# Edge stage of a graph layer: padding slots of the edge list get a row number past the table's end, and the row gathers skip them

## The chip, the cores and the metric

The kernel is one program on one core of a Trainium2 chip. The metric is the device time of one execution in microseconds (us). Three runs of the kernel before gave a median of 1887.54 us (1886.41 to 1888.28). All engine names are those of the profile: PE is TensorE's matmuls, PEld its weight loads, DVE VectorE, ACT ScalarE, POOL GpSimd, SP SyncE.

## The reference

A relational graph layer with a gate, then a mixture-of-experts layer (8 experts, top 2). Only the first concerns the change:

```python
# x [1250, 1024]; src, dst, edge_type [21250]; weight [8, 1024, 1024]
x = x + gnn(layernorm(x)); x = x + moe(layernorm(x))

def gnn(x):                                   # R = 8 relations
    out = x @ root + bias
    for r in range(8):
        mask = (edge_type == r)
        sums = segment_sum(x[src] * mask[:, None], dst)
        mean = sums / maximum(segment_sum(mask, dst), 1)[:, None]
        out = out + mean @ weight[r]          # = sum over edges of w_edge * (x @ weight[r])[src]
    z = concat([out, x], 1) @ w_gate + b_gate
    return tanh(out) * z + x * (1 - z)
```

## The kernel before, in words

The program has five blocks, one after the other, with a barrier of all engines between them.

1. The transform (0 to about 936 us). Y = x @ weight[r] for all 8 relations is computed and stored to device memory as a table of 8 x 1280 rows of 1024 floats (row number = relation * NP + node, NP = 1280). Each product is three matmuls, high and low parts in fp32r. Beside it DVE and PE sort the edges by destination block: each block of 128 destination nodes gets a stretch of slots that is padded to a multiple of 256 slots (GROUP = 2 tiles of 128). There are ET = 184 tiles of 128 slots, tile t being column t of `edge_row`, `edge_dst`, `edge_w` and `edge_key`. A slot without an edge is zero in all of them: its row number is 0, its destination number 0 (real ones are 1 to 128). About half way DVE computes these columns in a chain of small steps; then POOL fetches one weight (1/count) per slot with 184 small indirect DMAs from the table INV, and waits for the edge stage.
2. The edge stage (about 938 to 1356 us), the block of the change. Two things are interleaved in an order fixed by the generator `steps()`. "product" steps are four more half-width matrix products (root and the lower half of w_gate), 4 x 80 steps of 3 matmuls. "edges t" steps, one for every 1.7 products, add the rows of edge tile t to the accumulator: POOL gathers the 128 rows of Y that column t of `edge_row` names (one indirect DMA of 512 KB) into one of GR = 5 row buffers `gathered`; ACT multiplies by the edge weight and rounds to fp32r (`ghi`, HR = 3 buffers); DVE makes the rest (`glo`, written in place over the row buffer); PE multiplies both by a selection matrix `sel`, which holds a one where iota (1 to 128) equals the slot's destination number, 4 matmuls a tile; after every second tile DVE adds the result to the block's accumulator.
3. The gate and second layernorm, 4. routing, 5. the experts.

The five buffers are a ring. POOL may issue gather t when PE has finished tile t - 5 (semaphore `edge_tiles_used`), ACT waits for the landing (16 counts on `rows_gathered`), DVE for ACT (`rows_hi`), PE for DVE (`rows_lo`). SP, on its own queue, loads the weights of the next product (512 KB each) and stores the products YX.

The edges per block of destinations, counted from the inputs, are 2146, 2155, 2136, 2195, 2129, 2146, 2252, 2270, 2135 and 1686, together 21250. Blocks 0 to 8 take 18 tiles each and block 9 takes 14, so the blocks fill tiles 0 to 175, and tiles 176 to 183 hold nothing. Of the 23552 slots 2302 (9.8%) are padding. Tiles 17, 35, 53, 89, 107, 161 and 176 to 183 are padding alone, 14 tiles; ten tiles are so in part: 16 (30 of 128 slots), 34 (21), 52 (40), 71 (109), 88 (47), 106 (30), 125 (52), 143 (34), 160 (41) and 175 (106). All padding slots lie in the last partitions of their tile, and in the kernel before each of them fetches row 0 of Y.

Of the kernel before, what the change touches and what calls it, by code (L numbers as in the profile page):

```python
# [10 lines left out]
ALU = mybir.AluOpType  # L11
# [35 lines left out]
def build_program(nc, x, src, dst, edge_type, weight, root, bias, w_gate, b_gate,  # L47
                  gate_w, w1, w2, w3, out):
    s = shapes(x, src, weight, w1, gate_w)
    N, D, R, X, H, NT, NP, KC, HC = (s[k] for k in ("N", "D", "R", "X", "H", "NT", "NP", "KC", "HC"))  # L50
# [4 lines left out]
    assert ET % 4 == 0 and ECOLS >= EFULL + (EREST > 0) and HALF == BANK and D == 1024 and R == 8 and X == 8  # L55
    KEYS = NP * R
    BT = NT * R

    with ExitStack() as ctx:
        banks = ctx.enter_context(nc.psum_tensor("banks", [P, 8 * BANK], F32))  # L60
# [2 lines left out]
        def sem(name):  # L63
            return ctx.enter_context(nc.semaphore(name))
# [33 lines left out]
        edge_row = keep.put("edge_row", [P, ET], I32)  # L98
        edge_dst = keep.put("edge_dst", [P, ET], F32)
# [105 lines left out]
        oh_klo = z2b.put("oh_klo", [P, CPQ, P], BF16)  # L205
        oh_khi = z2b.put("oh_khi", [P, CPQ, BT], BF16)
        placed = z2b.put("placed", [P, 2, ET], F32)
        placed_i = z2b.put("placed_i", [P, 3, ET], I32)
        tfl = z2b.put("tfl", [P, 4, ET], F32)
        inv = z2b.put("inv", [P, BT], F32)  # L210
        YB, PLACE_BANK, COUNT_BANK = 4, psum[6], psum[7]
# [26 lines left out]
        with nc.Block() as block:  # L238
# [114 lines left out]
            def _(dve):  # L353
                v = nc.vector
# [6 lines left out]
                def columns(r, part, first=False):  # L361
# [5 lines left out]
                    def equal(out, n, column):  # L367
                        return v.tensor_tensor(out, iota[:, 0:n].unsqueeze(1).to_broadcast([P, CPQ, n]),
                                               column[:, at].unsqueeze(2).to_broadcast([P, CPQ, n]), ALU.is_equal)
# [6 lines left out]
                    equal(oh_lo[:], P, place_lo)  # L376
                    equal(oh_khi[:], BT, key_hi)
                    equal(oh_klo[:], P, key_lo)
# [129 lines left out]
                step = step1  # L508
                dve.wait_ge(cols_used, 8 * SORT_R)
                step(v.tensor_copy(placed[:], PLACE_BANK[:, 0:2 * ET].rearrange("p (a t) -> p a t", a=2)))  # L510
                step(v.tensor_scalar(inv[:], COUNT_BANK[:, 0:BT], 1.0, None, ALU.max))
                v.reciprocal(inv[:], inv[:]).then_inc(inv_ready, 1)  # L512
# [2 lines left out]
                step(v.tensor_copy(edge_dst[:], placed_i[:, 1]))  # L515
                step(v.tensor_scalar(placed_i[:, 2], placed_i[:, 0], R - 1, None, ALU.bitwise_and))
                step(v.tensor_copy(tfl[:, 0], placed_i[:, 2]))
                step(v.scalar_tensor_tensor(edge_row[:], tfl[:, 0], float(NP), placed[:, 0], ALU.mult, ALU.add))

                step(v.tensor_scalar(tfl[:, 1], iota[:, 0:ET], float(P), None, ALU.mult))  # L520
                step(v.memset(tfl[:, 2], 0.0))
# [4 lines left out]
                step(v.scalar_tensor_tensor(tfl[:, 3], tfl[:, 2], float(R), tfl[:, 0], ALU.mult, ALU.add))  # L526
                step(v.scalar_tensor_tensor(tfl[:, 1], edge_dst[:], float(BT), tfl[:, 3], ALU.mult, ALU.add))
                v.tensor_scalar(edge_key[:], tfl[:, 1], -float(BT), 0.0, ALU.add, ALU.max).then_inc(key_ready, 1)
                with dve.Fori(1 + SORT_R, R - 1) as r:
# [123 lines left out]
        GR, HR, SR, SG = 5, 3, 8, 4  # L653
# [9 lines left out]
        g_in = [sem(f"rows_gathered{i}") for i in range(GR)]  # L663
# [30 lines left out]
        with nc.Block() as block:  # L694
# [31 lines left out]
            @block.gpsimd  # L726
            def _(pool):

                for t in range(ET):
                    if t >= GR:  # L730
                        pool.wait_ge(g_used, t - GR + 1)
                    nc.gpsimd.indirect_dma_start(  # L732
                        out=gath[:, t % GR], out_offset=None, in_=Y,
                        in_offset=bass.IndirectOffsetOnAxis(ap=edge_row[:, t:t + 1], axis=0)).then_inc(g_in[t % GR], 16)

            @block.scalar
            def _(act):
# [885 lines left out]
```

## Time and profile before

| | |
|---|---|
| median of 3 runs | 1887.54 us (1886.41 to 1888.28) |
| the profiled execution, its own time | 1879.97 us |
| its span in the trace | 1877.9 us |
| granted TensorE clock, mean | 0.973 |
| PE busy | 1760.9 us, 94% |
| edge stage, share of the 16 DMA engines | about 83% |

The profile is of one execution. Times in the rows below count from the span's start. A matmul of 512 columns is shown as 0.39 us long although the next one starts 0.23 us after it, since matmuls are pipelined; idle time ahead of a matmul therefore begins only after those 0.39 us. Indirect DMAs are shown on POOL with the time in which their descriptors are written, not that of the transfer; the time from issue to landing is a column of its own.

### The profile page before, as it was taken

The page shows a single profiled execution, that of the slowest core. Times are in us where ns is not written, and L with a number is a line of the kernel's source. Part 1 is how long each engine was busy: PE and PEld are TensorE (multiplying, and loading weights), DVE is VectorE, ACT ScalarE, POOL GpSimd, SP SyncE. Part 2 cuts the span into 40 slices and gives each one's busy share as a digit, 9 for nine tenths or more (in the row PEclk, how much of TensorE's full clock was granted, in tenths as well). Part 3 has the DMA queues.
Part 4 walks back from the last instruction along what each step waited for, and adds up shares of the span by engine and source line. Part 5 has one row for each costly group of instructions (what it writes and reads, how often), then busy time and mean ns, then how long its engine had stood idle before and what let it go on. Part 6 is the DMA issues. An engine that isn't in the chain of part 4 may idle for free. (4 is left out here: it accounts for less than half of the span.)

```text
span 1877.9 us, 22607 instructions
## 1 busy us (share of the span) xinstructions
PE 1760.9 (94%) x8113; PEld 1448.1 (77%) x8113; DVE 962.8 (51%) x1166; ACT 595.3 (32%) x850; POOL 639.2 (34%) x535
## 2 busy tenths in 40 slices
PE   7999999999999999999999999999889967999993
PEld 6888888888888888888777777777668855787882
DVE  8545555655410110010079999998889976434300
ACT  2211111111111111111156656655532212455451
POOL 1000000000166666610055555555355523545531
PEclk9999999999999999999999999999989977999997
DMA  5222222222532222222188888888754445777645
GB/s 199 90 96 90 79 74 73 84 73 79 171 106 92 93 84 90 84 84 89 62 279 265 302 269 294 265 269 281 239 213 168 157 155 197 191 218 187 160 82 152
DMA packets 122552, 292.80 MB, mean 156 GB/s; under 512 B 16084, under 2 KB 32516, under 8 KB 122384
## 3 DMA queue, kind: packets, MB, share of 16 engines
q1 hardware_dynamic: 80592, 161.17, 24.3%
q0 software_dynamic: 41872, 130.44, 23.7%
q8 instruction: 57, 0.93, 0.2%
q14 instruction: 31, 0.25, 0.0%
HBM read 213.92 MB, written 82.76 MB: 158 GB/s over the span
## 5 line engine op out<-in xcount | busy, mean ns | idle before, releaser
L585 PE MATMUL banks<-whi,xhi 128*128 128x512 f32 x1280 | 502.0, 392 | 0.6 <-DVE xlo L473 0.6
L586 PE MATMUL banks<-wlo,xhi 128*128 128x512 f32 x1280 | 498.9, 390 | 0.0
L587 PE MATMUL banks<-whi,xlo 128*128 128x512 f32 x1280 | 498.9, 390 | 0.0
L732 POOL DMA_INDIRECT gathered<-Y,edge_row x184 | 220.8, 1200 | 317.5 <-PE banks L846 180.7
L309 ACT ACTIVATE y_out<-banks 128x512 f32<-128x512 f32 x160 | 95.5, 598 | 717.8 <-PE banks L587 717.8
L358 DVE TENSOR_TENSOR wlo<-w_stage,whi 128x1024 fp32r<-128x1024 f32 x66 | 80.7, 1224 | 459.6 <-ACT whi L301 458.9
L585 PEld LDWEIGHTS banks<-whi,xhi 128*128 128x128 f32 x1280 | 240.8, 188 | 50.6 <-DVE xlo L473 1.2
L587 PEld LDWEIGHTS banks<-whi,xlo 128*128 128x128 f32 x1280 | 240.7, 188 | 50.3
L586 PEld LDWEIGHTS banks<-wlo,xhi 128*128 128x128 f32 x1280 | 240.8, 188 | 49.0
L751 ACT ACTIVATE ghi<-gathered,edge_w 128x1024 fp32r<-128x1024 f32 x184 | 211.3, 1152 | 170.1 <-DMA gathered<-Y,edge_row 164.6
L789 DVE SCALAR_TENSOR_TENSOR glo<-gathered,edge_w,ghi 128x1024 fp32r<-128x1024 f32 x184 | 232.2, 1281 | 42.8 <-ACT ghi L751 42.3
L565 POOL DMA_INDIRECT edge_w<-INV,edge_key x184 | 181.2, 985 | 123.2 <-DMA edge_w<-INV,edge_key 102.6
L845 PE MATMUL banks<-ghi,sel 128*128 128x512 f32 x368 | 147.1, 400 | 19.5 <-DVE glo L789 19.3
L557 POOL DMA_DIRECT2D INV<-inv x1 | 0.6, 563 | 483.8 <-DVE inv L512 483.8
L846 PE MATMUL banks<-glo,sel 128*128 128x512 f32 x368 | 143.7, 390 | 0.0
L827 PE MATMUL banks<-whi,xhi 128*128 128x512 f32 x320 | 125.3, 391 | 3.2 <-PEq L238 3.2
L829 PE MATMUL banks<-whi,xlo 128*128 128x512 f32 x320 | 125.2, 391 | 0.0
L828 PE MATMUL banks<-wlo,xhi 128*128 128x512 f32 x320 | 125.2, 391 | 0.0
L799 DVE TENSOR_TENSOR acc<-acc,banks 128x1024 f32 x92 | 111.7, 1214 | 0.8 <-PE banks L846 0.7
L845 PEld LDWEIGHTS banks<-ghi,sel 128*128 128x128 f32 x368 | 69.0, 187 | 49.9 <-issue 37.1
L1537 PE MATMUL banks<-w13hi,xthi 128*128 x216 | 87.7, 406 | 0.8 <-issue 0.3
L1538 PE MATMUL banks<-w13lo,xthi 128*128 x216 | 85.2, 394 | 0.0
(254 smaller groups left out, 2385.5 us busy)
## 6 DMA issues: line engine op xcount, KB each, us to landing
Y<-y_out SPq DMA_DIRECT2D x160, 256.0 KB, 2.0
w_stage<-in_L_gnn_weight SPq DMA_DIRECT2D x62, 512.0 KB, 3.6
raw<-in_L_ffn_w SPq DMA_DIRECT2D x24, 1024.0 KB, 9.4
YX<-y_out SPq DMA_DIRECT2D x40, 256.0 KB, 5.1
w_stage<-in_L_gnn_w_gate SPq DMA_DIRECT2D x12, 512.0 KB, 7.0
X<-x SPq DMA_DIRECT2D x11, 512.0 KB, 3.0
acc<-in_L_gnn_bias POOLq DMA_DIRECT2D x10, 512.0 KB, 10.3
u<-YX SPq DMA_DIRECT2D x10, 512.0 KB, 5.0
```

The lines of the kernel that those rows point to most:

```text
L565: nc.gpsimd.indirect_dma_start(out=edge_w[:, t:t + 1], out_offset=None, in_=INV, in_offset=bass.IndirectOffsetOnAxis(ap=edge_key[:, t:t + ...
L585: pe.matmul(psum[slot][:], xhi[:, k, at], whi[h][:, k], start=(k == 0), stop=False)
L586: pe.matmul(psum[slot][:], xhi[:, k, at], wlo[h][:, k], start=False, stop=False)
L587: ins = pe.matmul(psum[slot][:], xlo[:, k, at], whi[h][:, k], start=False, stop=(k == KC - 1))
L732: nc.gpsimd.indirect_dma_start(out=gath[:, t % GR], out_offset=None, in_=Y, in_offset=bass.IndirectOffsetOnAxis(ap=edge_row[:, t:t + 1], a ...
L751: nc.scalar.activation(ghi[:, t % HR], gath[:, t % GR], ACT.Copy, scale=edge_w[:, t:t + 1]).then_inc(g_hi, 1)
L789: v.scalar_tensor_tensor(glo[:, t % GR], gath[:, t % GR], edge_w[:, t:t + 1], ghi[:, t % HR].bitcast(F32), ALU.mult, ALU.subtract).then_in ...
L827: pe.matmul(psum[j % 2][:], xhi[:, k, at], whi[0][:, k], start=(k == 0), stop=False)
L828: pe.matmul(psum[j % 2][:], xhi[:, k, at], wlo[0][:, k], start=False, stop=False)
L829: ins = pe.matmul(psum[j % 2][:], xlo[:, k, at], whi[0][:, k], start=False, stop=(k == KC - 1))
L845: pe.matmul(bank[:], sel[:, t % SR], ghi[:, t % HR, cols], start=start, stop=False)
L846: ins = pe.matmul(bank[:], sel[:, t % SR], glo[:, t % GR, cols], start=False, stop=stop)
```

## The change

Two steps are added to DVE's chain and one is altered: `edge_row` becomes relation * NP + source plus 2^20 where the destination number is 0. The gather gets a bound (the last row of the table, 10239) and `oob_is_err=False`, by which indices past the bound are left out instead of being an error. What a skipped slot's partition holds is then what the buffer held before: a finite value, multiplied by the weight of key 0 and selected by nobody, since the slot's destination number is 0. The weight gathers, the number of gathers, tiles and buffers are as before.

```diff
+    NO_ROW = 1 << 20
...
                 step(v.tensor_copy(tfl[:, 0], placed_i[:, 2]))
-                step(v.scalar_tensor_tensor(edge_row[:], tfl[:, 0], float(NP), placed[:, 0], ALU.mult, ALU.add))
+                step(v.scalar_tensor_tensor(tfl[:, 3], tfl[:, 0], float(NP), placed[:, 0], ALU.mult, ALU.add))
+                step(v.tensor_scalar(tfl[:, 2], edge_dst[:], 0.5, float(NO_ROW), ALU.is_lt, ALU.mult))
+                step(v.tensor_tensor(edge_row[:], tfl[:, 3], tfl[:, 2], ALU.add))
...
                     nc.gpsimd.indirect_dma_start(
                         out=gath[:, t % GR], out_offset=None, in_=Y,
-                        in_offset=bass.IndirectOffsetOnAxis(ap=edge_row[:, t:t + 1], axis=0)).then_inc(g_in[t % GR], 16)
+                        in_offset=bass.IndirectOffsetOnAxis(ap=edge_row[:, t:t + 1], axis=0),
+                        bounds_check=R * NP - 1, oob_is_err=False).then_inc(g_in[t % GR], 16)
```

On DVE, in the chain that follows the sort (transform stage), the order before was:

```order
391 L517 CAST tfl<-placed_i 128x184 [waits vector_step]
392 L518 SCALAR_TENSOR_TENSOR edge_row<-tfl,placed 128x184 [waits vector_step]
393 L520 TENSOR_SCALAR tfl<-iota 128x184 [waits vector_step]
394 L521 MEMSET tfl 128x184 [waits vector_step]
```

and in the changed kernel, at the same place, it is:

```order
391 L518 CAST tfl<-placed_i 128x184 [waits vector_step]
392 L519 SCALAR_TENSOR_TENSOR tfl<-tfl,placed 128x184 [waits vector_step]
393 L520 TENSOR_SCALAR tfl<-edge_dst 128x184 [waits vector_step]
394 L521 TENSOR_TENSOR edge_row<-tfl 128x184 [waits vector_step]
395 L523 TENSOR_SCALAR tfl<-iota 128x184 [waits vector_step]
396 L524 MEMSET tfl 128x184 [waits vector_step]
```

Two small instructions are new, each with a wait for the one ahead of it; all that follows on DVE keeps its order. On POOL, PE, ACT and SP the listed instructions and their order are the same. What the list does not show is that the bound is an operand in a register: in the built program one register move now stands ahead of each of the 184 gathers on POOL, and the wait for `edge_tiles_used` is on the move.

## Rows read from the trace of the kernel before

**Rows 1.** The page: busy time of each engine over the span.
```profile
PE 1760.9 (94%) x8113; PEld 1448.1 (77%) x8113; DVE 962.8 (51%) x1166; ACT 595.3 (32%) x850; POOL 639.2 (34%) x535
```
**Rows 2.** Windows over the edge stage: us, then busy (count), clock, DMA share, GB/s.
```profile
938.00:1147.00 209.00, 200.41 (x854) 159.38 (x855) 184.20 (x166) 121.28 (x119) 113.22 (x95) 0.99 0.85 279
1147.00:1252.00 105.00, 99.04 (x426) 78.47 (x425) 94.75 (x86) 60.52 (x60) 57.98 (x47) 1.00 0.85 282
1252.00:1356.00 104.00, 97.69 (x419) 77.31 (x417) 92.89 (x83) 58.77 (x58) 49.63 (x42) 1.00 0.79 257
```
**Rows 3.** Groups by line in 938 to 1356: busy us, mean ns, idle before and releaser.
```profile
L789 DVE SCALAR_TENSOR_TENSOR glo<-gathered,edge_w,ghi 128x1024 fp32r<-128x1024 f32 x184 | 232.2, 1281 | 42.8 <-ACT ghi L751 42.3
L732 POOL DMA_INDIRECT gathered<-Y,edge_row x184 | 220.8, 1200 | 317.5 <-PE banks L846 180.7 <-POOLq L238 130.6 <-issue 6.1
L751 ACT ACTIVATE ghi<-gathered,edge_w 128x1024 fp32r<-128x1024 f32 x184 | 211.3, 1152 | 170.1 <-DMA gathered<-Y,edge_row 164.6 <-PE banks L846 3.7
L845 PE MATMUL banks<-ghi,sel 128*128 128x512 f32 x368 | 147.1, 400 | 19.5 <-DVE glo L789 19.3
```
**Rows 4.** Waits, 938 to 1355: engine line, waited for, total us, times, longest.
```profile
PE banks L845 <- DVE glo L789: 19.3, 26, 2.3
```
**Rows 5.** The row gathers on POOL (ns), and their landing in us (min/median/max).
```profile
L732 POOL DMA_INDIRECT gathered<-Y,edge_row x184: 932/964/2273, 938.7 to 1345.1; - x184
DMA to landing us min/median/max: 4.3/5.8/9.2
```
**Rows 6.** Timeline of POOL, tile 4: start, us, row, idle before.
```profile
944.22 0.94 POOL L732 DMA_INDIRECT gathered<-Y,edge_row  x1 [0.30 <-issue]
```
**Rows 7.** Timeline of PE: first edge matmuls of a tile that came late.
```profile
965.71 0.47 PE L845 MATMUL banks<-ghi,sel 128*128 128x512 f32 x1 [0.85 <-DVE glo L789]
...
984.85 0.47 PE L845 MATMUL banks<-ghi,sel 128*128 128x512 f32 x1 [0.55 <-DVE glo L789]
...
1149.64 0.47 PE L845 MATMUL banks<-ghi,sel 128*128 128x512 f32 x1 [1.93 <-DVE glo L789]
...
1337.49 0.47 PE L845 MATMUL banks<-ghi,sel 128*128 128x512 f32 x1 [0.21 <-DVE glo L789]
```
**Rows 8.** Tile 17's gather on POOL, its landing, and that of tiles 178 to 183.
```profile
975.51 1.69 POOL L732 DMA_INDIRECT gathered<-Y,edge_row  x1 [1.33 <-PE banks L846]
...
gathered<-Y,edge_row POOLq DMA_INDIRECT x1, 6.7
...
gathered<-Y,edge_row POOLq DMA_INDIRECT x6, 5.6
```
**Rows 9.** The weight gathers: instruction times in ns, and landing in us.
```profile
L565 POOL DMA_INDIRECT edge_w<-INV,edge_key x184: 938/944/1926, 503.9 to 807.1; - x184
...
DMA to landing us min/median/max: 2.2/2.4/16.1
```
**Rows 10.** POOL's DMA queue in 938 to 1355: packets, MB, share of 16 engines.
```profile
q0 software_dynamic: 26496, 96.48, 71.2%
```
**Rows 11.** Timelines of SP and ACT where the third product's weights come late.
```profile
1138.41 0.38 SPq L702 DMA_DIRECT2D w_stage<-in_L_gnn_w_gate  x1
...
1145.36 1.06 ACT L745 ACTIVATE whi<-w_stage 128x1024 fp32r<-128x1024 f32 x1 [2.21 <-DMA w_stage<-in_L_gnn_w_gate]
```
**Rows 12.** Timeline of DVE: the altered step, and the tensor_scalar behind it.
```profile
491.50 0.35 DVE L518 SCALAR_TENSOR_TENSOR edge_row<-tfl,placed 128x184 int32<-128x184 f32 x1
491.88 0.26 DVE L520 TENSOR_SCALAR tfl<-iota 128x184 f32<-128x184 f32 x1
```
**Rows 13.** Groups by line, whole span: transform matmuls, DVE's splits, the scatter.
```profile
L585 PE MATMUL banks<-whi,xhi 128*128 128x512 f32 x1280 | 502.0, 392 | 0.6 <-DVE xlo L473 0.6
L358 DVE TENSOR_TENSOR wlo<-w_stage,whi 128x1024 fp32r<-128x1024 f32 x66 | 80.7, 1224 | 459.6 <-ACT whi L301 458.9
L1289 POOL DMA_INDIRECT X<-ye,add_i x27 | 50.9, 1884 | 49.4 <-DMA X<-ye,add_i 38.3 <-issue 11.1
```

## The prediction

> **What bounds the kernel now.** I read the busy shares first: PE is busy for 94% of the span [rows 1], so a change pays only if it takes matmuls away or closes gaps between them. This one takes none away: the padding tiles keep their four matmuls, their ACT and DVE steps and their gather instruction. So I went to the windows of the edge stage [rows 2]. There PE is busy 200.4 + 99.0 + 97.7 = 397.1 of 418 us, a gap of 20.9 us, and the DMA engines work for 79 to 85% of the time. That looks like a stage near its transfer limit; the waits tell otherwise. POOL idles 180.7 us for PE (ready to gather, no buffer free) and ACT 164.6 us for gathers [rows 3]: engines with time to spare. The wait that costs is PE's for `glo`, 19.3 us in 26 pieces, the longest 2.3 [rows 4]. That is 1.0% of the time, and all that any faster gather could give back.
>
> Why so little is lost: tiles come every 418 / 184 = 2.27 us, and the ring lets a gather be issued five tiles ahead, 11.4 us. A gather lands a median of 5.8 us after its issue [rows 5], then come ACT's 1.15 and DVE's 1.28 us [rows 3], together 8.2, and PE's four matmuls on tile t - 5, about 0.9 at 0.23 us each, before its buffer is free. That leaves 2.3 us, less what the signals between engines take and what DVE is held up by its additions: about 1.7 us of slack at the median landing, none near the longest of 9.2 us. The 26 late tiles are the tail of the landing times. They stand in 13 runs (members less than 11.4 us apart), the first late start at 965.71, the last at 1337.49 [rows 7].
>
> **The change, part by part.**
>
> *DVE's two added steps.* One TENSOR_SCALAR (0.26 us) and one two-input step that writes int32 (0.35 us, as the step it stands in for) [rows 12], about 0.65 us with the gaps between such steps, at 491.5 us. Behind them on DVE are the weight splits, ahead of which it idles 459 us in all, and the transform's first matmul line idles 0.6 us in total, for something else [rows 13]. POOL's 184 weight gathers wait too; the last starts at 807.1 [rows 9], and POOL then waits 130.6 us for the edge stage [rows 3]. Cost 0; 0.65 us if that cover were gone.
>
> *2302 rows fewer to move.* The gathers take 71.2% of the 16 engines over 417 us [rows 10], 297 / 184 = 1.6 us a tile. 9.8% of it is 29 us of engine time, nearly all in the 14 empty tiles and a few neighbours, and it helps only tiles in flight there. I held the late starts against the list of padding tiles. Tile 17 (all padding, issued at 975.51, landed after 6.7 us [rows 8]) started 0.55 us late at 984.85; that goes. Tile 175 (106 of 128 slots) started 0.21 late at 1337.49; that goes [rows 7]. The other 13 empty tiles were on time. One effect is indirect: at 1149.64 PE stood 1.93 us for tile 91, because ACT had waited 2.21 us for a weight transfer issued at 1138.41 [rows 7, 11]. It was queued behind tiles 88 and 89 (175 padding slots). At most one tile's 1.6 us of engine time was ahead of it, and tile 89 had mostly landed, so I take half, 0.8 us (ends 0 and 1.6). Sum of the skip: -0.55 - 0.21 - 0.8 = -1.6 us (ends -0.55 and -2.4).
>
> What an empty gather takes, no row shows. The nearest is the weight gather: as many slots, 4 bytes each, landing after 2.4 us against 5.8 [rows 9, 5], 3.4 us sooner. At either end an empty tile is early, and early is worth nothing, since PE takes tiles in order. By the Trainium skill (page "DMA: Bandwidth & Descriptors", section "Anatomy of one DMA — SWDGE (gpsimd) path") a DMA issued by GpSimd takes about 2.0 us plus its bytes at 436 GB/s. By that an empty tile is 1.2 us shorter, not 3.4, and a full one takes 3.2 us where the trace has 5.8; the rows don't bear its numbers out under this load. With its 1.2 in place of my 0.8 ahead of the weight transfer the sum would be 0.4 us lower.
>
> *The bound, on all 184 gathers.* Two prices. First the register move: it carries the wait now, so it and the gather start only after PE's signal. No row shows a register move on POOL; the nearest is the 0.30 us between back-to-back gathers [rows 6], which holds the hand-over of a whole instruction. So 0 to 0.30 us; I take 0.05, a small part of that. Second, 128 comparisons while descriptors are written. Weight and row gathers take the same 0.94 us at their shortest whatever they fetch [rows 9, 5], about 7 ns a slot. The lower end is below nothing: if skipped slots write no descriptor, an empty tile's instruction shortens by up to 0.94 us, on 14 tiles alone. The upper end is the scatter at the program's end, another kind of indirect DMA, with a mean of 1.88 us against the row gathers' 1.20 [rows 13, 3], +0.68. I take +0.05, since the nearest rows don't differ at all. So 0.1 us of added latency on each gather (ends about 0 and 0.98).
>
> What is 0.1 us worth? It is paid only where a tile is late. A late tile holds PE 0.1 longer, but the tiles already issued then gain what PE lost, so it is paid once a run at least and once a late tile at most: 13 x 0.1 to 26 x 0.1. The rest have slack. I take +1.3 us.
>
> **Sum.** 0 - 1.6 + 1.3 = -0.3 us. On the profiled execution: 1879.97 - 0.3 = 1879.7. The median of the runs stands 7.57 us above it and nothing here scales with that: 1887.54 - 0.3 = 1887.2 us. No change, then; a difference below 0.2% (3.8 us) is about what can't be told from none here.
>
> **Rivals.**
>
> *The bounded gather is a slower path on POOL (slower).* It takes as much longer as the scatter, +0.68 us, and most of the 0.30 for the move [rows 13, 6]: +0.9. For: it is another form of the instruction, with a register operand, and the trace has indirect DMAs of both lengths. Against: two forms with different sources cost the same. The slack of 1.7 us shrinks to 0.8, the known late tiles cost 13 x 0.9 = 12 to 26 x 0.9 = 23 us, and new late ones join. I take +14, less the skip's 1.6: 1900 us. It decides from +0.4 us a gather on (13 x 0.4 = 5.2, less 1.6). Its harsh form: if each gather took as long as the longest before, 2.27 us, and 0.30 between them [rows 5, 6], POOL would need 2.57 x 184 = 473 us for a stage of 418: +55 us, 1942 us.
>
> *The skip relieves the ring more than I count (faster).* Tiles 17, 91 and 175 lose their whole lateness, 0.55 + 1.93 + 0.21 = 2.7 us [rows 7], and the lighter queue takes as much again from late tiles near padding: 5.4 us, 1882 us. For: over 80% of the DMA engines' time is used here. Against: the last six gathers, all padding, landed after 5.6 us [rows 8], no later than others, so reading row 0 again and again was no hot spot whose end helps; and most late starts lie far from padding. All 19.3 us would give 1868.
>
> *The change doesn't do what it says.* Slots past the bound are still fetched, clamped to the last row. The bytes stay and only the +1.3 us remain: 1888.8 us, no change either.
>
> **How the numbers follow.** Forecast, small costs and small savings: 0.56, own range 1884.5 to 1891. Not skipped: 0.05, also no change. Slower path: 0.25 mild (1891.4 to 1905), 0.04 harsh. Faster: 0.10. So faster by over 0.2% 0.10, within 0.61, slower 0.29. For 8 in 10 the range goes from 1884 to 1900: it leaves out about 0.07 below, and the harsh form with the mild one's upper part, 0.12, above.
>
> **What the profile after would show.** The gather on POOL: a median within 0.1 us of 964 ns says the bound is cheap, 1.3 us or more that the rival is right. Landing: the median still about 5.8 us, the minimum 2.9 or less (the empty tiles); a minimum above 4 would say that nothing is skipped. POOL's DMA queue in the stage: 2302 packets fewer if a skipped slot writes none. PE's wait for `glo`: 17 to 21 us, without late starts at tiles 17 and 175. DVE: two more instructions near 491 us and nothing else moved; the edge stage begins at 938 us as before. I am wrong if PE's wait for `glo` passes 24 us or falls below 15, or if another stage changes its length by over 1 us.

## The result and the profile after

The changed kernel is slower: over 14 runs of each on the same chips the ratio to the kernel before is 1.0052 (95% interval 1.0028 to 1.0075), some 10 us. The medians of all 14 are 1900.22 and 1888.40 us; four runs of the changed kernel (1956 to 1962 us, at a granted clock of 0.95 to 0.96 against 0.97) and two of the kernel before (1941 and 1953 us) are left out of the ratio (medians without them 1896.80 and 1888.22), and since the first profile of the changed kernel caught one of these four, the rows of "after" are those of a second measurement. The second measurement, beside the experiments below, gave 1895.50 against 1882.49, ratio 1.0064 (1.0045 to 1.0082), some 12 us. The forecast was no change, 1887.2 with a range up to 1900, and a chance of 0.29 for slower. The profiled execution of after took 1895.69 us, 15.7 more than that of before; 1879.97 is a short execution of the kernel before, so not all of the 15.7 is the change's.

The waits of the edge stage come first, in the columns of [rows 4]; they answer to [rows 3, 4]:

```profile
POOL gathered L735 <- PE banks L850: 168.8, 128, 5.5
ACT ghi L755 <- DMA gathered<-Y,edge_row: 167.5, 121, 8.1
POOL gathered L735 <- POOLq L239: 132.0, 1, 132.0
DVE glo L793 <- ACT ghi L755: 55.7, 57, 5.4
PE banks L849 <- DVE glo L793: 30.7, 41, 3.1
POOL gathered L735 <- issue: 27.7, 55, 3.3
```

PE's wait for `glo` is 30.7 us in 41 pieces, before 19.3 in 26. That is 11.4 of the 15.7 us. Most of the rest lies in waits too short for this view, since idle time starts only behind the 0.39 us that a matmul is drawn with. Counted from start to start in the timeline (what goes beyond 0.23 us between the first matmul of a tile and the one ahead of it), 38 tiles are late before, by 25.3 us, and 53 after, by 39.3: 14.0 of the 15.7. The third row, POOL waiting 132.0 us for the stage to begin, is 130.6 before: the transform is untouched. The last row is new in size: 27.7 us in 55 pieces in which POOL stood idle and, by the profile, PE's signal was not what ended it, before 6.1 us [rows 3]. In 51 of them the signal had come while the gather ahead was still being written, and 34 of these gathers started later than the 0.30 us after it that they keep otherwise (tile 8 below is one).

The gathers and their landing after, to be held against [rows 5]:

```profile
L735 POOL DMA_INDIRECT gathered<-Y,edge_row x184: 984/998/2603, 939.0 to 1361.1; - x184
DMA to landing us min/median/max: 2.1/5.6/8.9
```

Writing the descriptors takes 52 ns more at the least (984 against 932) and 34 more at the median. Landings are no later, and the shortest is 2.1 us instead of 4.3: the empty tiles (with the same gathers and nothing skipped, in an experiment below, it is 4.3 again). The stage starts at 939.0 (before 938.7), but its last gather is issued at 1361.1 instead of 1345.1. The whole loss lies in this stage.

The DMA queues of the stage (938 to 1370; before in [rows 10]):

```profile
q0 software_dynamic: 26496, 87.06, 63.8%
```

9.42 MB less, which is 2302 rows of 4096 bytes, and as many packets as before. The sizes of the packets say what became of them: before 23552 of 4096 bytes and 2944 of 4 bytes, after 21250 and 5246. So a skipped slot still costs a packet, of 4 bytes.

So the skip works as described and the time is lost between PE and POOL. The timeline shows it. First PE, the first matmul of tiles 0 to 3 in the changed kernel, then POOL's gathers of tiles 5 to 8, which wait for exactly these four tiles:

```profile
946.43 0.47 PE L849 MATMUL banks<-ghi,sel 128*128 128x512 f32 x1 [1.06 <-DVE glo L793]
...
948.85 0.47 PE L849 MATMUL banks<-ghi,sel 128*128 128x512 f32 x1
...
951.23 0.39 PE L849 MATMUL banks<-ghi,sel 128*128 128x512 f32 x1
...
952.82 0.39 PE L849 MATMUL banks<-ghi,sel 128*128 128x512 f32 x1
```

```profile
948.38 1.18 POOL L735 DMA_INDIRECT gathered<-Y,edge_row  x1 [2.71 <-PE banks L850]
950.80 0.99 POOL L735 DMA_INDIRECT gathered<-Y,edge_row  x1 [1.24 <-PE banks L850]
953.09 1.11 POOL L735 DMA_INDIRECT gathered<-Y,edge_row  x1 [1.30 <-PE banks L850]
954.68 0.99 POOL L735 DMA_INDIRECT gathered<-Y,edge_row  x1 [0.48 <-issue]
```

From PE's start on tile t - 5 to the gather of tile t it is 1.95, 1.95, 1.86 and 1.86 us (the 0.09 more stand where PE's first matmul of the tile is one of 0.47 us). In the kernel before it is 1.34 us for the same four; two rows of each:

```profile
946.35 0.39 PE L845 MATMUL banks<-ghi,sel 128*128 128x512 f32 x1
...
950.88 0.39 PE L845 MATMUL banks<-ghi,sel 128*128 128x512 f32 x1
```

```profile
947.69 1.30 POOL L732 DMA_INDIRECT gathered<-Y,edge_row  x1 [2.53 <-PE banks L846]
...
952.22 1.22 POOL L732 DMA_INDIRECT gathered<-Y,edge_row  x1 [1.33 <-PE banks L846]
```

Every gather that waits for a buffer is issued 0.52 us later behind PE's signal. This holds over the whole stage: from the start of the fourth matmul of tile t - 5, whose end gives the signal, a gather that PE releases starts 0.66 or 0.67 us later before (167 of 169), and 1.18 or 1.19 us after (124 of 128).

The trace has the register moves too:

```profile
L735 POOLq MOVE  x184: 29/29/29, 938.2 to 1360.3; - x184
```

The move for tile 5 starts at 947.63, 0.43 us behind PE's fourth matmul of tile 0 at 947.20, and takes 29 ns; the gather starts at 948.38, 0.75 us behind the start of the move. In 154 of the 179 rounds it is 0.76 us.

### The profile page after: what moved, and what is told of

Same layout as the page of the kernel before. It is cut to its first block and busy times, and to the rows that moved or that the text cites. A ratio compares the mean times of both kernels' runs of the same rounds, so it can differ in the third digit from the quotient of the medians.

```text
span 1956.7 us, 22793 instructions
## 1 busy us (share of the span) xinstructions
PE 1784.3 (91%) x8113; PEld 1451.7 (74%) x8113; DVE 964.7 (49%) x1168; ACT 594.9 (30%) x850; POOL 644.0 (33%) x535
## 5 line engine op out<-in xcount | busy, mean ns | idle before, releaser
L735 POOL DMA_INDIRECT gathered<-Y,edge_row x184 | 227.9, 1239 | 400.4 <-POOLq L239 203.8
L568 POOL DMA_INDIRECT edge_w<-INV,edge_key x184 | 176.9, 962 | 116.0 <-DMA edge_w<-INV,edge_key 77.9
```

The costliest lines, as they stand in the source:

```text
L568: nc.gpsimd.indirect_dma_start(out=edge_w[:, t:t + 1], out_offset=None, in_=INV, in_offset=bass.IndirectOffsetOnAxis(ap=edge_key[:, t:t + ...
L735: nc.gpsimd.indirect_dma_start(out=gath[:, t % GR], out_offset=None, in_=Y, in_offset=bass.IndirectOffsetOnAxis(ap=edge_row[:, t:t + 1], a ...
```

## The experiments

Theory A: the register move that now carries the wait delays each gather by about 0.5 us, and the ring's thin slack turns that into time. Rivals: the bound check is slow (B), or the time comes from outside the stage (C).

**The changed kernel again** (no edit).

> The changed kernel once more, for an undisturbed profile on the same chip as the runs below. Theory A (the register move that carries the wait delays each gather, about 0.5 us between PE's signal and the start of the gather on POOL, since the gather no longer stands ready behind its own wait): 5 to 12 us over the kernel before, PE's wait for glo 27 to 32 us in 35 to 40 pieces, back-to-back gathers on POOL about 0.06 us longer each. Theory B (checking the bound makes descriptor writing itself slower or lands the rows later): the same total, but the gather's start after PE's signal is as before and its row on POOL is 0.5 us longer. Theory C (nothing in the edge stage; the long time is disturbance of other stages): edge stage 415 to 417 us as before.

Measured: ratio 1.0064 (1.0045 to 1.0082). The rows above are its; the wait for `glo` is 30.7 us in 41 pieces, much as A says, and B's signs (a late landing, a long row on POOL) are absent. C falls, since the first and last gathers bound the loss.

**The bound in a register set once**, rows still skipped:

```diff
+                bound_reg = nc.alloc_register(mybir.EngineType.Pool, "bound")
+                nc.gpsimd.reg_mov(bound_reg, R * NP - 1)
+                bound = nc.gpsimd.snap(bound_reg)
                 for t in range(ET):
                     if t >= GR:
                         pool.wait_ge(g_used, t - GR + 1)
...
-                        bounds_check=R * NP - 1, oob_is_err=False).then_inc(g_in[t % GR], 16)
+                        bounds_check=bound, oob_is_err=False).then_inc(g_in[t % GR], 16)
```

The wait stands on the gather itself again.

> Bound put in a register once before the loop, so that no register move stands ahead of the gathers and each gather carries its own wait again; padding rows still skipped. Theory A: back to the time of before, -2 to +1.5 us of it, PE's wait for glo 17 to 22 us. Theory B (the bound check itself costs): as slow as the changed kernel, +5 to +12 us.

Measured: 1881.42 against 1882.49, ratio 0.9991 (0.9980 to 1.0002); the whole loss is gone. Its PE and POOL rows for tiles 0 and 5 are 1.34 us apart, as in the kernel before:

```profile
946.59 0.39 PE L852 MATMUL banks<-ghi,sel 128*128 128x512 f32 x1
```

```profile
947.93 1.16 POOL L738 DMA_INDIRECT gathered<-Y,edge_row  x1 [2.51 <-PE banks L853]
```

```profile
PE banks L852 <- DVE glo L796: 20.8, 29, 2.0
```

Its profiled execution took 1885.59 us, 5.6 more than that of before, and the 5.6 lie between first and last gather (938.8 to 1350.9). The runs beside each other don't show them, so a part of the 15.7 above is how short that one execution of before was.

**Bound and register moves, nothing skipped**: the changed kernel with the one step for `edge_row` as before.

```diff
-                step(v.scalar_tensor_tensor(tfl[:, 3], tfl[:, 0], float(NP), placed[:, 0], ALU.mult, ALU.add))
-                step(v.tensor_scalar(tfl[:, 2], edge_dst[:], 0.5, float(NO_ROW), ALU.is_lt, ALU.mult))
-                step(v.tensor_tensor(edge_row[:], tfl[:, 3], tfl[:, 2], ALU.add))
+                step(v.scalar_tensor_tensor(edge_row[:], tfl[:, 0], float(NP), placed[:, 0], ALU.mult, ALU.add))
```

> The changed gathers, bound and register moves included, but row numbers as before, so that no index is past the bound and all 23552 rows are moved. Theory A: slow as the changed kernel or 1 to 2 us slower, +6 to +14 us over before: what skipping gives back is the difference, predicted as 1.6 us. Rival (the skipped slots themselves cost, by small packets or by a branch on POOL): as fast as before.

Measured: ratio 1.0076 (1.0061 to 1.0091), 14 us, the upper end of what was expected: slow without any skipped slot, so the skipped slots are not what costs.

**Bound set once, nothing skipped**: both edits together.

> Bound in a register set once, row numbers as before: the price of the bound check alone, with all rows moved. Theory A: 0.06 us a gather, +0.5 to +2 us, hardly told from none. Theory B: +5 to +12 us.

Measured: ratio 1.0013 (0.9999 to 1.0027), +2.4 us, not surely different from none. With this the four corners stand: moves with skip 1.0064, moves without 1.0076, set once with skip 0.9991, set once without 1.0013. The moves cost 0.0073 and 0.0063 of the time (13.7 and 11.9 us); the skip gives back 0.0012 and 0.0022 (2.3 and 4.1 us), each with an uncertainty of 3 to 5 us, so that a gain is likely and its size open.

**Register moves ahead of the wait.** Is it the move, or its place?

```diff
+                bound_reg = nc.alloc_register(mybir.EngineType.Pool, "bound")
                 for t in range(ET):
+                    nc.gpsimd.reg_mov(bound_reg, R * NP - 1)
+                    bound = nc.gpsimd.snap(bound_reg)
                     if t >= GR:
                         pool.wait_ge(g_used, t - GR + 1)
...
-                        bounds_check=R * NP - 1, oob_is_err=False).then_inc(g_in[t % GR], 16)
+                        bounds_check=bound, oob_is_err=False).then_inc(g_in[t % GR], 16)
```

> As the changed kernel, but two register moves stand ahead of the wait in each round, and the gather itself carries the wait. Theory A1 (what costs is that an instruction ahead of the gather carries the wait, so that the gather is not ready when PE's signal comes): as fast as the kernel with the bound set once, -3 to +2 us of before; gather starts 1.34 us after PE's start on tile t - 5. Rival A2 (the moves' own time, or a register rewritten just before its use, costs): as slow as the changed kernel, +10 to +14 us, start at 1.86 us.

Measured: ratio 0.9993 (0.9981 to 1.0004). Two moves a gather, and no cost: they run ahead of the wait, and a gather starts 1.34 us after PE's start again. A2, by which the moves themselves cost, falls.

**Another instruction that carries the wait**, in the kernel before, with no bound and no register:

```diff
+                apart = sem("wait_apart")
                 for t in range(ET):
                     if t >= GR:
                         pool.wait_ge(g_used, t - GR + 1)
+                        pool.sem_inc(apart, 1)
```

> The kernel before, with one semaphore increment (of a semaphore that nobody waits for) between the wait and the gather: no bound, no register, no skip; the increment carries the wait. Theory A1: slow like the changed kernel with all rows moved, less the bound's 2 us: +8 to +13 us, gather start at about 1.8 us instead of 1.34. Rival A3 (special to register moves): -1 to +2 us, start at 1.4 us or less.

Measured: ratio 1.0070 (1.0050 to 1.0090), +13 us, the upper end of what was expected. A3, by which only register moves do this, falls. PE's first matmul of tile 0 and POOL's gather of tile 5, and of tiles 1 and 6, are 1.88 us apart:

```profile
947.40 0.39 PE L847 MATMUL banks<-ghi,sel 128*128 128x512 f32 x1
...
949.66 0.39 PE L847 MATMUL banks<-ghi,sel 128*128 128x512 f32 x1
```

```profile
949.28 1.12 POOL L734 DMA_INDIRECT gathered<-Y,edge_row  x1 [4.34 <-PE banks L848]
951.54 0.94 POOL L734 DMA_INDIRECT gathered<-Y,edge_row  x1 [1.15 <-PE banks L848]
```

This is the plainest run of all: nothing of the change is in it but that the wait is not on the gather, and it costs what the change costs. Its wait for `glo` in the view is smaller (24.4 us in 32 pieces), but by the starts 52 tiles are late by 32.9 us, and from first to last gather it is 420.0 us against 406.4 before.

**Two moves between wait and gather.**

```diff
+                bound_reg = nc.alloc_register(mybir.EngineType.Pool, "bound")
                 for t in range(ET):
                     if t >= GR:
                         pool.wait_ge(g_used, t - GR + 1)
+                    nc.gpsimd.reg_mov(bound_reg, R * NP - 1)
+                    bound = nc.gpsimd.snap(bound_reg)
...
-                        bounds_check=R * NP - 1, oob_is_err=False).then_inc(g_in[t % GR], 16)
+                        bounds_check=bound, oob_is_err=False).then_inc(g_in[t % GR], 16)
```

> As the changed kernel, but two register moves between the wait and the gather instead of one. If the cost is that the gather is not ready at the signal, a second move adds only its own few tens of ns: gather start 1.86 to 1.95 us after PE's start on tile t - 5, time +10 to +15 us over before. If each move costs 0.5 us, the start is at 2.35 us and the time +24 to +30 us.

Measured: ratio 1.0055 (1.0037 to 1.0074), no slower than with one. Tile 0's matmul and tile 5's gather:

```profile
946.63 0.39 PE L852 MATMUL banks<-ghi,sel 128*128 128x512 f32 x1
```

```profile
948.56 0.99 POOL L738 DMA_INDIRECT gathered<-Y,edge_row  x1 [3.12 <-PE banks L853]
```

1.93 us, 0.07 more than 1.86. The moves' own time is small. Where, then, do the 0.52 us go? The moves of the changed kernel answer it, at the start of the stage, where nothing waits for PE:

```profile
L735 POOLq MOVE  x5: 29/29/29, 938.2 to 940.4; - x5
```

They follow each other 0.54 to 0.59 us apart, with one gather between them, while the gathers' own rows on POOL follow about 1.3 us apart or more. So POOL takes the instructions in well ahead of running them, and one gather costs it about 0.51 us there beside the 0.03 of the move. With two moves it is 0.60 to 0.65. A gather that carries the wait can have this behind it when the signal comes; one behind the waiting instruction begins it then, and 0.51 fits the 0.52. That the two are the same thing is a reading of these rows; no run takes it apart further.

**Four row buffers**, to see what the delay is worth with less slack: `GR, HR, SR, SG = 4, 3, 8, 4` in place of 5, 3, 8, 4, in the kernel before, in the changed one, and in the one with the bound set once.

> The kernel before with four row buffers in place of five. If the ring's slack (about 1.7 us at the median landing) is what hides the gathers, taking 2.27 us of it away makes the ring the bound: a cycle of about 1.34 + 6.0 + 1.4 + 1.4 = 10.1 us for four tiles, 2.53 us a tile, 184 x 0.26 = +48 us in all, less the 29 us or so that the late tiles cost already: +20 to +45 us. If something else than the ring makes tiles late (ACT's or DVE's order), under +8 us.

> The changed kernel with four row buffers. With the ring as the bound each 0.52 us more between signal and gather is paid once in four tiles: 46 x 0.52 = 24 us more than the kernel before with four buffers, +0.06 us a gather for the bound 3 us, less 2 to 5 us for the rows skipped: 20 to 27 us above it. Rival (the delay costs only where a tile happens to be late, however deep the ring): 10 to 14 us above it, as with five buffers.

> Four row buffers, rows skipped, bound in a register set once. The changed kernel with four buffers was 14 to 16 us above the kernel before with four, where I had expected 20 to 27. Theory D1 (the late signal costs its 0.5 us once in four tiles, 24 us, and skipping gives back some 10 us with a ring this tight): this kernel stands about 10 us below the kernel before with four buffers (ratio to the kernel before near 1.025). Theory D2 (the delay costs 26 to 30 tiles' worth as with five buffers, about 14 us, and the skip and the bound are even): equal to the kernel before with four buffers, ratio near 1.030.

Measured against the kernel before with five: 1.0300 (1.0285 to 1.0315), 1.0385 (1.0370 to 1.0401) and 1.0264 (1.0236 to 1.0291); medians 1940.65, 1954.37 and 1933.38 us. My +20 to +45 for the first was too low (+56): I had subtracted what late tiles cost already, and without that the sum was +48. That the tail of the landings comes on top is likely and not tested. The wait for `glo` in the kernel before with four buffers (whole span):

```profile
PE banks L845 <- DVE glo L789: 63.1, 76, 4.0
```

The second stood 14 us (medians) to 16 us (ratios) above it, not 20 to 27, which left two readings; the third speaks for one. Between the changed kernel with four buffers and the same with the bound set once lie 21 us by the medians, 22.8 by the ratios, against 46 x 0.52 = 24: with the ring as the bound the delay is paid once a round. The profiled stages say the same: from first to last gather the changed kernel's row below has 482 us, and with the bound set once it is 458 (939.1 to 1397.2).

```profile
L735 POOL DMA_INDIRECT gathered<-Y,edge_row x184: 984/1086/2027, 938.6 to 1420.6; - x184
```

Skipping, bound check included, now gives 7 us back, where with five it gives some 2. With four runs of each the intervals of 1.0300 and 1.0264 still overlap a little (1.0285 to 1.0315, 1.0236 to 1.0291). D1 holds in kind; its 10 us were 7.

**The bound set once, again**, as the version that might beat the kernel before.

> The kernel with the bound set once and rows skipped, a second time, as the candidate for a version that beats the kernel before: -1 to -3 us if the 0.9991 of its first measurement holds, 0 if that was noise.

Measured: 1884.12 against 1884.29, ratio 0.9990 (0.9975 to 1.0005). Three measurements of two kernels of this kind (the bound set once, twice, and the moves ahead of the wait) gave 0.9991, 0.9993 and 0.9990, each with 1 just inside its interval. A gain of about 0.1% is likely and not shown by any one of them. No version clearly better than the kernel before was found.

## Why the prediction was wrong

**What bounds the stage**: right. PE loses nearly all its time where `glo` is late, and the change's cost showed up in that wait: 30.7 us, past the 24 that the prediction named as a sign of being wrong. The number was too small: 19.3 us in 26 pieces is what the view shows, 25.3 us in 38 what the starts of the matmuls give.

**DVE's two steps**: right, nothing moved (first gather at 939.0 against 938.7).

**Skipped rows**: about right in size, and by luck. I took 1.6 us; the pairs give 2.3 and 4.1, uncertain by 3 to 5 us. Minimum landing 2.1 us as foreseen, bytes down by 9.42 MB; packets did not go down, which I had left open. But the three terms of the sum did not come. Tile 17 is on time in the changed kernel, and as much on time with nothing skipped. Tile 175, whose 0.21 us were to go, is late by 0.41 in the changed kernel and by 0.38 with the bound set once. And the 0.8 us ahead of the weight transfer was not there: tile 91 is 1.93 us late as before. Tiles 91 and 175 after:

```profile
1155.17 0.47 PE L849 MATMUL banks<-ghi,sel 128*128 128x512 f32 x1 [1.93 <-DVE glo L793]
...
1352.98 0.47 PE L849 MATMUL banks<-ghi,sel 128*128 128x512 f32 x1 [0.41 <-DVE glo L793]
```

The wait ahead of ACT's weight splits, before 6.3 us in two pieces, is now

```profile
  DMA w_stage<-in_L_gnn_w_gate: 7.2, 2
```

Where the 2 to 4 us of the pairs come from stays open.

**The bound check on POOL**: right. +0.05 us was taken and 52 ns measured at the minimum; alone it makes +2.4 us with an interval that includes none.

**The register move**: this is the step that failed. "So 0 to 0.30 us; I take 0.05": it was 0.52. I saw that the move carries the wait, and priced the move. The bound I drew was from back-to-back gathers, 0.30 us apart [rows 6], and those don't wait for anything, so the row could not show what an unready instruction costs after a signal: in the changed kernel, with a move between them, the same gathers are still 0.30 us apart. The trace of before had a nearer row. The first gather of the stage, at 938.72, stands behind the two semaphore instructions of the barrier, which hold the wait there:

```profile
L238 POOLq EVENT_SEMAPHORE  x2: 17/17/17, 937.8 to 937.9; - x2
```

It starts 0.80 us after the second of them (937.92), far past my 0.30. With 0.52 in place of 0.05, and the bound's 0.05, it makes 0.57 us a gather.

**What a delay is worth**: this term was too small as well. I took one payment for each of 13 runs of late tiles, with 26 late tiles as the other end. The moves' measured 11.9 and 13.7 us over 0.52 are 23 and 26 payments, near the upper end. With the right price and my 13 payments the sum would have been 13 x 0.57 - 1.6 = +5.8 us; with 26 x 0.57 = 15 and 3 us for the skip it is +12, which is what was measured. That agreement is found afterwards, and 26 is no true upper end: 38 tiles are late by their starts, and the delay makes new late ones, 53 in all.

**The rivals.** The slower one had a fitting threshold (+0.4 us a gather) and a fitting result (1900), but its mechanism, a slow descriptor path, is not what happened: the path is 0.05 us longer, and the delay lies ahead of it. I had given the move "most of the 0.30" within it and the larger part to the path: 0.57 us a gather against 0.9, and more payments than it counts, come out at the same time by luck. The faster rival wanted tiles 17, 91 and 175 on time and 5.4 us less; 91 and 175 are late, and with the bound set once the time is under 2 us less. That nothing would be skipped is refuted by the bytes.

## What to carry to other kernels

When an edit gives an instruction a new operand in a register, look at which instruction then carries the wait. A gather behind a register move or a semaphore increment that holds the wait started 0.5 us later here than one that holds it itself; put such work ahead of the wait, or outside the loop. What a delay on a ring costs can be estimated from the count of late pieces at the consumer times the delay (here 23 to 26 payments for 26 pieces in the view), and where the ring is the bound, from the number of rounds. Saving transfers where the consumer is not waiting gives little: 9.8% of the rows gone here were worth 2 to 4 us of 1888, with an uncertainty as large.

## What the runs showed of the hardware that I had not expected

- On POOL, an indirect DMA that carries its own semaphore wait starts 0.52 to 0.54 us sooner after the signal than one behind another instruction that carries it (1.34 against 1.86 to 1.88 us from PE's start), and it makes no difference whether that is a register move or a semaphore increment. A second register move adds 0.07 us. The waiting move itself takes 29 ns, and the gather starts 0.76 us behind its start; where nothing waits, the moves follow each other 0.54 us apart with a gather between them.
- An index past the bound still takes a packet (26496 in the stage with and without), of 4 bytes in place of 4096, and an indirect DMA with all 128 slots past it lands after 2.1 us at the least, against 4.3 for the shortest full one.
- The bound check adds 52 ns to the writing of 128 descriptors (984 against 932 ns), with or without skipped slots. Why the kernel with the bound set once still has single gathers up to 2.65 us long (before: 2.27) stays open.
